# Joining every even attention unit to the next in TensorE's order, in a one-core differential-attention and FFN kernel

## What is computed

```python
xn = layernorm(x)
q1, k1, q2, k2, v = split(xn @ Wqkv)        # 16 heads; q, k of 8 columns a head, v of 16
A1 = causal_softmax(q1 @ k1.T / sqrt(8)) @ v
A2 = causal_softmax(q2 @ k2.T / sqrt(8)) @ v
d  = A1 - lam * A2
d  = (1 - LAMBDA_INIT) * d / sqrt(mean(d * d) + 1e-5)      # over the 16 columns of a head
ffn = fp8(gelu(fp8(xn) @ Wg0) * (fp8(xn) @ Wg1)) @ fp8(Wl)
out = x + d @ Wproj + ffn
```

## Time and profile before

| | us |
|---|---|
| three runs, lowest / median / highest | 184.03 / 184.3 / 184.45 |
| the profiled execution: its own time | 184.12 |
| the profiled execution: its span | 182.3 |
| TensorE matmul busy | 175.5 (96%) |
| ScalarE busy | 163.2 (90%) |
| VectorE busy | 92.4 (51%) |
| GpSimd busy | 63.5 (35%) |
| TensorE's granted clock, mean | 0.999 of full speed |

### The profile page before, as it was taken

One profiled execution on the slowest core, in us unless ns is written; L12 is line 12 of the kernel. 1 busy time (PEld: TensorE's weight loads), 2 busy tenths in 40 slices (PEclk: granted clock), 3 DMA queues, 4 the chain that ended last, 5 costly groups with the idle time before them and its releaser, 6 DMA issues.

```text
span 182.3 us, 4305 instructions
## 1 busy us (share of the span) xinstructions
PE 175.5 (96%) x1816; PEld 76.3 (42%) x1816; DVE 92.4 (51%) x219; ACT 163.2 (90%) x146; POOL 63.5 (35%) x81
## 2 busy tenths in 40 slices
PE   6999999999999999999999999999999999989992
PEld 6785344543332333343234434334524434432481
DVE  1878789312233230640374121706542789979982
ACT  3586678999999999999999999999999999999820
POOL 8449920052017322360622063217303560323000
PEclk9999999999999999999999999999999999999999
DMA  5996888780000000000277875000000000000015
GB/s 152 382 333 227 219 197 201 175 189 19 0 0 5 0 0 4 0 4 0 42 204 179 210 173 127 0 0 4 4 0 0 4 0 4 0 0 4 0 58 180
DMA packets 8935, 15.02 MB, mean 82 GB/s; under 512 B 2000, under 2 KB 5584, under 8 KB 8912
## 3 DMA queue, kind: packets, MB, share of 16 engines
q1 hardware_dynamic: 8080, 13.92, 28.0%
q10 hardware_dynamic: 832, 0.79, 1.3%
HBM read 5.26 MB, written 1.05 MB: 35 GB/s over the span
## 4 chain that ended last, share of the span: by engine, by line
PE 82%; DVE 11%; ACT 2%; DMA 2%; issue 1%; DVEq 0%
PE ps L1062 35%; PE ps L1050 20%; PE ps L904 12%; PE ps L970 7%; PE ps L1098 4%; DVE o_t L719 2%; PE ps L914 2%; DMA x_sb<-L_attn_x 2%; DVE parts L625 1%; PE ps L894 1%; PE ps L1103 1%; DVE parts L737 1%; ACT L455 1%; DVE area L630 1%; DVE xn_t L763 1%
## 5 line engine op out<-in xcount | busy, mean ns | idle before, releaser
L497 ACT ACTIVATE probs<-ps,shift 128x1536 f32<-128x1536 f32 (+1 forms) x97 | 138.1, 1582 | 0.2 <-PE ps L1050 0.2
L1062 PE MATMUL ps<-probs,v_all 128*32 128x512 f32 (+3 forms) x776 | 78.1, 492 | 1.0 <-DVE o_t L719 0.8
L393 POOL TENSOR_SCALAR_AFFINE_SELECT probs<-probs 128x1024 f32<-128x1024 f32 (+1 forms) x40 | 36.7, 918 | 94.9 <-ACT probs L497 94.8
L1050 PE MATMUL ps<-q_st,k_st 32*128 32x512 f32 (+3 forms) x384 | 48.3, 411 | 0.0
L1050 PEld LDWEIGHTS ps<-q_st,k_st 32*128 32x128 f32 x384 | 22.5, 182 | 61.5 <-ACT probs L497 43.4
L719 DVE STREAM_TRANSPOSE o_t<-ps 128x512 f32<-128x512 f32 x16 | 11.5, 717 | 45.0 <-PE ps L1062 45.0
L1062 PEld LDWEIGHTS ps<-probs,v_all 128*32 128x32 f32 x776 | 16.4, 108 | 18.7 <-issue 9.7
L970 PE MATMUL ps<-area 128*128 128x512 fp8e4 x64 | 14.4, 379 | 0.2 <-DVE parts L625 0.2
L473 ACT ACTIVATE probs<-ps 128x512 bf16<-128x512 f32 x16 | 9.6, 597 | 3.7 <-PE ps L970 3.1
L644 DVE TENSOR_TENSOR area<-ps,probs 128x512 fp8e4<-128x512 f32 x16 | 10.9, 685 | 1.9 <-ACT probs L473 1.7
L970 PEld LDWEIGHTS ps<-area 128*128 128x128 fp8e4 x64 | 6.0, 98 | 8.0 <-issue 0.8
(11 more groups left out here) (90 smaller groups left out, 126.5 us busy)
## 6 DMA issues: line engine op xcount, KB each, us to landing
q_st<-parts SPq DMA_DIRECT2D x32, 128.0 KB, 2.8
k_st<-parts SPq DMA_DIRECT2D x32, 128.0 KB, 2.8
probs<-L_ffn_w_gating SPq DMA_DIRECT2D x4, 512.0 KB, 7.6
probs<-L_ffn_w_linear SPq DMA_DIRECT2D x1, 1024.0 KB, 12.4
out<-probs SPq DMA_DIRECT2D x3, 256.0 KB, 2.3
x_sb<-L_attn_x ACTq DMA_DIRECT2D x2, 256.0 KB, 5.1
w_q<-L_attn_Wqkv SPq DMA_DIRECT2D x1, 512.0 KB, 9.4
w_q<-L_attn_Wqkv SPq DMA_DIRECT2D x1, 256.0 KB, 4.2
```

Source lines behind the costliest of these rows:

```text
L393: pool.affine_select(out=blocks, in_=blocks, pattern=pattern, compare_op=ALU.is_ge, fill=0.0, base=0, channel_multiplier=-1).then_inc(mask ...
L497: act.activation(probs[:, at:at + PER_UNIT, cols], ps[:, 3 * (n % 2):3 * (n % 2) + 3, cols], ACT.Exp, bias=shift[:, br, 1, hg * BR + br:hg ...
L1050: ins = pe.matmul(ps[:, bank, at:at + wide * P], k_st[rows, g % STACKS, kb * P:(kb + 1) * P], q_st[rows, g % STACKS, queries], start=True, ...
L1062: ins = pe.matmul(ps[32 * j:32 * j + 32, 6, q0 % HALF:q0 % HALF + wide * P], v_all[:, g % HG, kb, 32 * j:32 * j + 32], probs[:, slot + j, ...
```

## The change

It makes four edits.

1. `JOINED` holds all even units from 0 to 88. In the unit loop the program goes on to the next unit's scores right behind the scores of a joined unit, and does the values and the side work of both behind the second. Units 90 to 95 stay as they were.
2. In the opening of attention, `project_values(1)` moves from unit 0's side work to before the first scores.
3. On VectorE, the conversion of the second half of the normalized input to fp8 (`x_to_fp8(1)`) moves behind the last two splits of the first queries and keys (`rest(2)`, `rest(3)`).
4. The ending: TensorE does the residual of block 6 and the p = 0 projections of blocks 6, 2, 3, 4, 5 and 7 before it waits for `out_t_ready` 3, and the p = 1 projections of 0, 1, 2, 3 come after; `turn_back(1, 0, 16)` becomes two halves, the second behind `difference(3, 1)`; the DMA of block 7 moves from SyncE's queue to ScalarE's, behind block 6's.

```diff
-V_AT = {0: (1, 2), 1: (3,), 2: (4,), 3: (5,), 4: (6,), 5: (7,)}
+V_AT = {0: (2,), 1: (3,), 2: (4,), 3: (5,), 4: (6,), 5: (7,)}
...
+JOINED = set(range(0, 90, 2))
...
             for b in (2, 4):
                 sp.wait_ge(y_added, b // 2)
                 sp.dma_start(out_rows[:, b:b + 2, :], y[:, b:b + 2, :]).then_inc(y_out, 16)
-            sp.wait_ge(y_added, 3)
-            sp.dma_start(out_rows[:, 7, :], y[:, 7, :]).then_inc(y_out, 16)
             sp.wait_ge(y_out, 16 * 5)
...
             whole(6)
             act.wait_ge(y_copied, 3)
             act.dma_start(out_rows[:, 6, :], y[:, 6, :]).then_inc(y_out, 16)
+            act.wait_ge(y_added, 3)
+            act.dma_start(out_rows[:, 7, :], y[:, 7, :]).then_inc(y_out, 16)
...
             rest(1, QK_BANK[1])
-            x_to_fp8(1)
             rest(2, QK_BANK[2])
             rest(3, QK_BANK[3])
+            x_to_fp8(1)
...
             scale_by_root(2, all_of)
-            turn_back(1, 0, 16)
+            turn_back(1, 0, 8)
             take(7, 1)
             difference(3, 1).then_inc(ms_ready, 1)
+
+            turn_back(1, 8, 8)
             dve.wait_ge(rms_ready, 1)
...
                     pe.wait_ge(hidden_ready, 14)
                     project_values(0)
+                    project_values(1)
                 for n in range(n0, n0 + BRANCH):
                     scores(n, general)
-                    values_due(n, HG if general and br == 1 else 0, GROUPS)
-                    beside(n)
+                    if n in JOINED:
+                        continue
+                    for m in (n - 1, n) if n - 1 in JOINED else (n,):
+                        values_due(m, HG if general and br == 1 else 0, GROUPS)
+                        beside(m)
...
                 values_due(UNITS, 0, GROUPS)
                 values_due(UNITS + 1, 0, GROUPS)
+                pe.wait_ge(res_ready, TB // 2)
+                residual(6, start=True)
+                project(6, 0)
+                project(2, 0, start=True)
+                project(3, 0)
+                project(4, 0, start=True)
+                project(5, 0)
+                project(7, 0, start=True)
                 pe.wait_ge(out_t_ready, 3)
                 project(0, 1)
                 project(1, 1).then_inc(y_ready, 1)
-                project(2, 0, start=True)
-                project(3, 0)
+                pe.wait_ge(out_t_ready, 4)
                 project(2, 1)
                 project(3, 1).then_inc(y_ready, 1)
-                project(4, 0, start=True)
-                project(5, 0)
-                project(7, 0, start=True)
-                project(6, 0, start=True)
-                pe.wait_ge(res_ready, TB // 2)
-                residual(6)
-                pe.wait_ge(out_t_ready, 4)
+                pe.wait_ge(out_t_ready, 5)
                 project(4, 1)
                 project(5, 1).then_inc(y_ready, 1)
-                pe.wait_ge(out_t_ready, 5)
+                pe.wait_ge(out_t_ready, 6)
                 for b in (6, 7):
                     project(b, 1).then_inc(y_ready, 1)
```

## The result

| | before | after |
|---|---|---|
| median of the runs, us | 184.32 (4 runs, 184.03 to 184.45) | 194.37 (4 runs, 194.27 to 194.74) |
| profiled execution: time / span, us | 184.12 / 182.3 | 194.74 / 193.0 |
| ratio after to before | | 1.0551, 95% interval 1.0532 to 1.057 |

The account below looks back on a forecast made before the run. ScalarE's pace of 1.431 us a unit was taken as the bound, TensorE only tying. 184.12 + 0.56 (opening) + 7.0 (attention: 3.2 + 4.2 - 0.4) + 1.0 (ending) = 192.7 us, range 189.4 to 195.2.

Parts of the forecast that it names:

- ScalarE's pace bounds the attention: Attention: exponentials end every 1.431 us, TensorE only ties, so a faster TensorE can win 0.4 us there.
- The ordinary joint, 0.15 per two pairs: Attention: odd scores wait for exponential m-2 with both values blocks behind; four units take 5.87 instead of 5.72, 3.2 us.
- rival B: Attention: scores behind an idle TensorE start slower by their weight load, 0.10 to 0.16 more each, 194.9 to 196.1; chance 0.14.
- Rival A: Attention: only the taken joints cost, ordinary joints are hidden; 189.5 us; chance 0.14.
- The taken joints, 6 times 0.69: Units 8, 20, 32, 44, 56, 78: VectorE's take stands inside the double values block, 2.55 instead of 1.86; 4.2 us.
- joint 40: Attention, unit 40: left out of the count of ordinary joints, as it has only the norms beside.
- The opening, 0.56: Opening: moved conversion delays the first gated product and FFN step 3, 0.1 to 0.7, taken as 0.6; +0.56 with unit 0's joint.
- The ending, 1.0: Ending: blocks 0 and 1 come later, the root and the chain behind it follow, block 7's DMA issues at 180.55 against 179.55; +1.0.
- The root behind the copies: Ending: ScalarE copies blocks 0 and 1 before the root, which ends at 176.92 instead of 175.28, about 1.65 later.
- the move between queues: Ending: block 7's DMA on ScalarE's queue instead of SyncE's, worth 0.3 us, inside the ending's sum.
- low bound for the ending: Ending: if the copies did not block the root, 0.5 us faster than today.

Follow-up runs that it names:

- the two split versions: Kernel before with only turn_back(1, 0, 16) halved and TensorE's projections reordered around it: 184.49 us; the same with block 7's DMA on ScalarE's queue: 184.41 us.
- The two runs with half values: Every values product over half its columns: on the kernel before 183.78 us profiled (other execution 189.46), on the changed kernel 192.88 and 194.37 us.

## Why the prediction was right, step by step

The mechanism held in all three stretches; the ending's size did not.

- **ScalarE's pace bounds the attention.** Shown in one execution: 133.10 us with TensorE busy 18% less.
- **The ordinary joint, 0.15 per two pairs.** The place and the size held: the late exponentials are 4, 8, 14, 18, 26, 30 and so on, by 0.12 to 0.16, fifteen times, 2.1 us; the joints at 82 and 86, whose second unit ends in 128x128 matmuls, cost 0.35 each. 2.8 against the 3.2 of the sum. Scores that start on an idle TensorE begin 0.05 behind the exponential and take 0.50: rival B is out. Rival A is out by these 2.8.
- **The taken joints, 6 times 0.69.** Five came at 0.71 to 0.82, 3.8 us in all. At unit 46 it was 1.22, through a step that the prediction didn't have: the norms of unit 41 behind the values of 40, so that VectorE's chain reached into the take. The prediction counted joint 40 as free, since its block is short. It is free for ScalarE and not for VectorE. With the six undone, taking this joint out gave 1.0 us of attention back; in the changed kernel, where unit 44 is joined too, unit 46 is only about 0.5 later than the other five. Together 5.0 against 4.2 (six times 0.69 is 4.1, not the 4.2 of the sum). With the 2.8 that is 7.8 over the pace, and 7.5 over the kernel before, whose small stalls (0.4) are gone. That the attention came out near its 7.0 is in part luck: the ordinary joints were 0.4 under, the taken ones 0.8 over.
- **The opening, 0.56.** The moved conversion is 0.55, shown by putting it back. The prediction's range for it was 0.1 to 0.7, and its choice of 0.6, then 0.56, is not worked out; that it hit is luck in the size. The other 0.55 of the profiled execution lies before anything that the change touches: ScalarE's first L436 starts at 12.71 in it and at 12.17 before. TensorE's matmuls were slow for longer. The 20 warm-up matmuls took 4.63 us, 3.88 in the kernel before and in the run with the conversion back (timelines of the changed kernel and of that run), which puts the first transposes 0.22 later, and these took 0.27 longer to the next matmuls.

```profile
1.61 4.63 PE L903 MATMUL ps<-ident 128*128 128x128 f32 x20 [1.61 <-POOL ident L336]
```
```profile
1.61 3.88 PE L903 MATMUL ps<-ident 128*128 128x128 f32 x20 [1.61 <-POOL ident L336]
```

  It is chance and no part of the change: two other executions of the same program up to there (six joints undone, block 7 on SyncE) have L436 at 12.17 and 12.20. The warm-up isn't the only thing that varies there; the run with the conversion back has the short one and L436 at 12.46. It is probably one reason why the profiled run is 0.4 above the others.
- **The ending, 1.0.** The root behind the copies: 1.61 late against 1.65 forecast; the last issue starts 10.88 behind the end of exponential 94 against 9.91 before, 0.97 against 1.0. What the sum lacked is the issue itself: 1.28 instead of 0.50, and 0.3 more from its end to the end of the wait. The prediction took the issue's length for fixed and gave the move between queues 0.3; no run shows a gain from it. The term is 2.0 in the profiled execution and 1.7 to 1.9 in the five others with this ending, not 1.0. The prediction's low bound for the ending, 0.5 faster than today with the root in time, did not hold either: with the root first the last issue does start 0.47 earlier, and the ending is 0.7 longer than before, by the same long issue.

So the terms of the sum that were mis-sized are the ending (by 1.0) and unit 46 (by 0.5); 0.55 is TensorE's slower start in the profiled execution.

**What stays open:** why the last issues are long. They vary from one execution of the same ending to the next: with that of the changed kernel and full values products, block 7's took 0.68 to 1.28 us, and that of blocks 4 and 5 took 0.37 where block 7's took 0.80 or 1.28, and 1.29 to 1.57 in the others. Where issues of blocks 4 and 5 on SyncE's queue and of block 7 on ScalarE's overlapped (six runs), they ended within 0.05 of each other. Counted from the issue of blocks 2 and 3, the long one ends after 1.8 to 2.0 us when blocks 0 and 1 were issued 3.7 to 4.0 before (before, and the two split versions), 2.0 to 2.6 when 2.5 before (the changed kernel and those with its ending), and 2.75 to 2.8 when 1.0 before (the two with the root first). The two runs with half values do not fit: 2.3 us where the first group has 1.8 to 2.0, and 1.75 where the second has 2.0 to 2.6. It may be waiting for earlier output to leave; no run took a transfer away.

## What to carry to other kernels

When two engines tie, take the pace from a stretch in which one of them is ahead, and ends from ends; the chain names the wrong engine. A reordering that saves time on the engine that isn't the bound must still be walked around the loop of buffers: start from the event that frees a bank and add every instruction that stands between it and the next write, a neighbour engine's answer included. In an in-order program, moving work earlier on one engine (14 matmuls here, block 6's residual and six projections) delays what stands behind its result on another (the root behind two copies).

## What the runs showed that was not expected

- ScalarE's records begin earlier and earlier while their ends keep the pace: 2.23 us long at unit 94 with half values, 1.54 at unit 1, ends 1.431 apart. Their starts are no measure of the work.
- TensorE's granted clock, 1.00 in the joined kernel with full values, fell to the level of 1.2 GHz with halved ones (0.50 over the 4 us from 98), after TensorE had been idle for more of each pair (0.93 at a time); in the unjoined kernel with halved values, busy 108 of 133 us in smaller pieces, it stayed at 1.00 in the profiled execution, but its other execution had a mean of 0.917. With full values products the clock fell once, in the kernel with only six units joined, where TensorE had idled 0.90 and 0.40 just before and within the joint. So the idle time is a likely reason and not shown to be one. Four such dips stand in the joined kernel's profile, and the exponentials in them were up to 1.5 us late.
- A DMA issue of 128 KB at the end took 0.37 to 1.40 us of the issuing engine's time, and block 7's 0.68 to 1.28 with the same code.
- Two small steps of VectorE, 0.15 us by themselves, ended only with the GpSimd mask that ran beside them, up to 0.78 us after their start, and made an exponential on ScalarE 1.2 us late.
